# A two-layer graph kernel on one core: one-hot spans of 11 nodes per tile for 12

## What is computed

```python
deg = segment_sum(1, dst); mean(v) = segment_sum(v, dst) / max(deg, 1)
# layer 0
msg = (x[src] + rel_emb[type]) @ W_msg.T + b_msg
x   = layernorm(x + x @ W_self.T + b_self + mean(msg))
# layers 1 and 2, residual around both
h   = swish(mean(x[src]) @ W1_l.T + b1 + x @ W1_r.T)
out = layernorm(x + mean(h[src]) @ W2_l.T + b2 + h @ W2_r.T)
```

## Time and profile before

| | before |
|---|---|
| median of three runs | 349.58 us (349.37 to 349.80) |
| the profiled execution | 349.91 us, span 348.1 us |
| busy: TensorE | 326.0 us, 94% of the span |
| TensorE weight loads | 243.2 us |
| VectorE | 229.0 us, 66% |
| ScalarE | 176.7 us, 51% |
| GpSimd | 4.9 us |
| granted clock, mean | 0.99 |
| count of the first group starts | 11.33 us |
| last count ends | 167.74 us |

### The profile page before, as it was taken

How to read it: one execution, slowest core, us unless ns; L and a number is a source line. 1 busy time by engine, 2 the same in 40 slices (tenths; PEclk the granted TensorE clock), 3 DMA queues, 4 the chain that set the end, 5 groups by cost and what they waited for, 6 DMA issues and landing times.

```text
span 348.1 us, 9071 instructions
## 1 busy us (share of the span) xinstructions
PE 326.0 (94%) x3322; PEld 243.2 (70%) x3322; DVE 229.0 (66%) x592; ACT 176.7 (51%) x389; POOL 4.9 (1%) x18
## 2 busy tenths in 40 slices
PE   1689999999999999999999999999999999999990
PEld 0688799999999999999884654564564554554560
DVE  6989999999999999999337963303306315315404
ACT  3596787779779879779422431321332411220220
POOL 5000000000000000000000000000000000000000
PEclk9989999999999999999999999999999999999997
DMA  5702000000000000000200000000000011011011
GB/s 147 237 18 78 2 2 3 8 4 4 8 2 5 6 5 6 5 2 3 76 12 1 2 0 0 2 0 2 0 2 1 3 30 30 2 30 31 2 32 37
DMA packets 6957, 7.29 MB, mean 21 GB/s; under 512 B 653, under 2 KB 5888, under 8 KB 6912
## 3 DMA queue, kind: packets, MB, share of 16 engines
q1 hardware_dynamic: 6624, 6.25, 6.0%
q10 hardware_dynamic: 288, 0.43, 0.5%
HBM read 4.75 MB, written 1.60 MB: 18 GB/s over the span
## 4 chain that ended last, share of the span: by engine, by line
PE 87%; DVE 7%; ACT 1%; issue 1%; ACTq 0%; DVEq 0%
PE ps L1049 38%; PE ps L1030 18%; PE ps L975 18%; PE ps L1121 5%; PE ps L1131 3%; DVE hot L1286 2%; PE ps L1068 2%; DVE hot L1279 1%; PE ps L982 1%; DVE table L1296 1%; PE ps L992 1%; PE ps L1096 1%; ACT sum_first L828 1%; DVE table L1286 0%; PE ps L1012 0%
## 5 line engine op out<-in xcount | busy, mean ns | idle before, releaser
L1049 PE MATMUL ps<-counts,table 128*128 128x512 f16 (+1 forms) x736 | 135.2, 340 | 0.0
L910 ACT CAST counts<-ps 128x494 f32 x208 | 107.5, 576 | 33.5 <-PE ps L975 32.6
L1049 PEld LDWEIGHTS ps<-counts,table 128*128 128x128 f16 x736 | 60.6, 97 | 64.8 <-DVE table L1415 0.2
L1030 PE MATMUL ps<-counts,table 128*128 128x256 f16 x600 | 80.0, 271 | 1.0 <-ACT sum_first L828 0.8
L975 PE MATMUL ps<-hot 128*128 128x156 f16 (+1 forms) x592 | 67.7, 240 | 7.8 <-DVE hot L1286 7.6
L975 PEld LDWEIGHTS ps<-hot 128*128 128x128 f16 x592 | 53.1, 102 | 11.4 <-DVE hot L1286 9.6
L1286 DVE TENSOR_TENSOR hot<-iota,edges 128x1200 f16<-128x1200 f16 x74 | 57.3, 774 | 0.0
L1030 PEld LDWEIGHTS ps<-counts,table 128*128 128x128 f16 x600 | 52.0, 96 | 6.6 <-issue 1.3
L1279 DVE TENSOR_TENSOR hot<-iota,edge_rows 128x768 f16<-128x768 f16 x74 | 40.5, 548 | 3.1 <-PE ps L1012 2.7
L982 PE MATMUL ps<-window_hot,hot 128*128 128x19 f16 x296 | 42.5, 179 | 0.0
L851 ACT ACTIVATE scaled<-ps,rdeg 128x128 f32<-128x128 f32 (+1 forms) x75 | 21.7, 373 | 24.0 <-PE ps L1121 21.6
(11 more groups left out here) (149 smaller groups left out, 328.2 us busy)
## 6 DMA issues: line engine op xcount, KB each, us to landing
own_T<-x_turned SPq DMA_DIRECT2D x4, 256.0 KB, 2.6
table<-x_rows SPq DMA_DIRECT2D x1, 832.0 KB, 5.8
table<-x_rows SPq DMA_DIRECT2D x1, 768.0 KB, 4.2
out<-new_first SPq DMA_DIRECT2D x3, 256.0 KB
out<-hot SPq DMA_DIRECT2D x3, 256.0 KB, 2.3
sum_first<-x_turned SPq DMA_DIRECT2D x2, 256.0 KB, 4.4
counts<-counts SPq DMA_DIRECT2D x6, 53.0 KB
counts<-first_dst ACTq DMA_DIRECT2D x1, 208.0 KB, 3.6
```

The lines of the kernel that those rows point to most:

```text
L910: nc.scalar.copy(A[:, HALVES[half], bass.ds(bases[group % 8], GROUP_W)], window(group, half)).then_inc(copied[half], 1)
L1030: last = nc.tensor.matmul(ps[:, sums_bank(q), at:at + PART], table0[:, b, which, :], A[:, b, part * PART:(part + 1) * PART], start=k == 0, ...
L1049: last = nc.tensor.matmul(ps[:, sums_bank(q), 0:nodes], table[:, b, which, :], A[:, b, at:at + nodes], start=b == which == 0, stop=b + 1 = ...
```

## The change

TILE_W becomes 11. With it a tile's (block, node) row is 275 columns for 300 (L1286: 1100 for 1200 in a group), the block matmuls stream 143 and 132 columns for 156 and 144, `iota` has 550 elements for 600, MOST_SHIFT is 27 for 26, and the limits of the checks follow. A group's pair row is 531 columns for 556. `hot` then has 2124 words of four bytes for `later`, which held 2216; so `steps` (104 words) moves into `edge_rows`, and the last bias and the stacked identity move down by 104 words. With three lines added, line numbers behind it are larger by 3.

```diff
-TILE_W = 12
+TILE_W = 11
...
         checks = later[:, 4 * D + 2 * CHUNK:4 * D + 2 * CHUNK + TILES]
-        steps = later[:, 4 * D + 2 * CHUNK + TILES:4 * D + 2 * CHUNK + TILES + GROUPS]
-        bias_last = later[:, 4 * D + 2 * CHUNK + TILES + GROUPS:][:, 0:D]
-
-        ident_stacked = later[:, 5 * D + 2 * CHUNK + TILES + GROUPS:].bitcast(F16)[:, 0:LAST]
-        assert 5 * D + 2 * CHUNK + TILES + GROUPS + P // 4 <= (SLOTS - 1) * HOT_C * GROUP // 2
+        bias_last = later[:, 4 * D + 2 * CHUNK + TILES:][:, 0:D]
+
+        ident_stacked = later[:, 5 * D + 2 * CHUNK + TILES:].bitcast(F16)[:, 0:LAST]
+        assert 5 * D + 2 * CHUNK + TILES + P // 4 <= (SLOTS - 1) * HOT_C * GROUP // 2
+
+
+        edge_room = edge_row[:].rearrange("p h k t -> p (h k t)")
+        steps = edge_room[:, 2 * CHUNK:2 * CHUNK + 2 * GROUPS].bitcast(F32)
```

## The result

347.69 us is the median of six runs of the changed kernel (347.34 to 348.42), 349.48 that of six runs of the kernel before beside them (348.97 to 350.83): ratio 0.9953, 95% interval 0.9938 to 0.9968. The change is faster by 1.8 us. 345.4 was forecast with a range from 344.3 to 347.1: the sign was right, the size was not, and the range missed. The profiled execution took 347.51 us for a span of 345.6.

A forecast was written before the change was run, and what follows sets the result against it. TensorE was taken to bound the loop from 39.34 us, VectorE mostly before. Loop 3.35 plus start 0.9 gives 4.25, say 4.2 us off a 349.91 us profiled execution: 345.7, shifted 0.33 to the median, 345.4 us; range 344.3 to 347.1.

The forecast's parts named there:

- TensorE's count of a group: Counting loop: eight block matmuls lose 100 columns, 42 ns a group; over 87 groups 3.65 us.
- the sign that I had set for success: Trace of the count: the 128x143 matmul followed after 65 ns, with a count of 0.69 us.
- the loop's sum: TensorE-bound loop from group 17 on: 3.65 us by columns less 0.30 hidden by ScalarE, giving 3.35 us.
- What ScalarE keeps back of it: Loop: waits for ScalarE's copies hide three groups' saving, 0.13 us, and four at the share matmul, 0.17 us.
- The start: Before 40 us: VectorE's rows 0.58 plus TensorE's counts 0.55 less 0.22 for the low clock, 0.9 us.
- VectorE's part: One-hot rows, 53 ns less a group: worth nothing by itself where TensorE bounds, but needed to leave VectorE room.
- Parts at nothing: Moved steps and constants, shorter iota, pair row no longer a multiple of 16 bytes: all taken as zero cost.
- (a): Rival, loop: weight loads from uneven rows take half as long again, 78 ns a group; 352.1 us, 5%.
- (b): Rival, loop: written PSUM runs, not columns, set TensorE's pace, so only VectorE's 0.6 us stays; 349.0 us, 4%.
- (c): Rival, early chunks: ScalarE takes more, 25 groups gain nothing, 1.05 us for 0.30; 346.1 us, 12%.
- (d): Rival, before 40 us: the clock falls once more, giving back up to 1.7 us; 347.1 us, 5%.

The follow-up runs named there:

- e11: Kernel before with spans of 10 nodes, rows kept at 2224 bytes, leaving out the edge beyond; 343.69 us (one run).
- e3: Kernel before with spans of 8 nodes, rows kept at 2224 bytes, leaving out the edges beyond; 339.15 us (one run).
- e1: Changed kernel with one unused column between pair rows, pitch 2128 bytes for 2124; 347.55 us, ratio 0.9944 to the kernel before.
- e12: Kernel before, spans of 12, each tile's place rounded down to an even column; 348.18 us, ratio 0.9949 to the kernel before.
- e15: e1 with each tile's place rounded down to an even column; 346.68 us, ratio 0.9918 to the kernel before.
- e6: e1 with lighter ScalarE: early chunks' messages scaled by one instruction for four tiles, normalising cut to two columns; 346.65 us (one run).
- e5: TensorE alone narrowed to 11, VectorE still writing 1200 columns, rows 2224 bytes; 347.66 us, ratio 0.9945 to the kernel before.
- e2: Kernel before with one unused column between pair rows, pitch 2228 bytes for 2224, widths unchanged; 350.73 us (one run).
- e10: e1 with constant, mostly odd places (0, 9, 17, 25) instead of registers, so counts are wrong; 347.14 us (one run).
- e16: e15 with the four relation matmuls grouped behind the first half's four block matmuls; 346.31 us, ratio 0.9907 to the kernel before.

## Why the prediction was wrong, point by point

**The step that failed** is "TensorE's count of a group": eight block matmuls lose 100 columns at 0.42 ns, "I take 42". The slope came from matmuls that write contiguous columns. It nearly holds among even widths (38 and 39 ns for 100 columns in the medians of e11 and e3), but the step from 12 to 11 gives less. By the table of odd places, each odd place costs the kernel before 13 ns, two matmuls at 6.5; with 1.7 odd places in a group that is 23 ns above 702. At 11 columns a run has one odd end wherever it lies: at even places the count is 689 and not 702 - 42 = 660, so 29 ns are lost, and odd places add 6 each, 11 in all. With both ends called edges, these cost 23 ns before and 40 after; 42 - 17 = 25, and 728 - 702 = 26 is what e1 shows. Of the 42 ns, then, some 17 go to the edges, 2 to the pitch (a mean of 714 in e1, 716 after), about 7 to waits (the mean lies 5 ns above the median before, 12 after), and 17 were kept, as far as such differences add up.

What the runs show is the 29 ns, and the effect of the place; that the odd end is what costs the 29 is my inference. e11's runs of 10 have no odd end at even places, and there it gives back 68 ns for 200 columns (634 for 702), 16 short of 84. Against the middle of its even neighbours, 668 ns, 11 columns lose 21; the other 8 are open. Spacing by spacing, from e12 to e15, with all places even, the eight block matmuls give 27 ns (541 to 514, sums of median spacings) and the six short ones behind them take 16 back (159 to 175). So the sign that I had set for success, a 128x143 matmul followed after 65 ns, came nearly true (66) and told little: half of the loss sits behind the next matmul.

**Against the loop's sum.** 86 x 42 ns = 3.6 us were to be had by columns. Edges take 86 x 17 ns = 1.46, the pitch 0.2 (126.26 less 126.05), 1.31 were gained; some 0.6 are left, for which I had 0.30. "What ScalarE keeps back of it" was right for the share matmul: 0.2 us in the same four groups (0.47 to 0.67 us in the change), for 0.17. Another 0.2 us is lost in the five groups with late matmuls, where the prediction had nothing, and 0.1 us between the counts, where L1033's waits for ScalarE rose from 0.8 to 1.2 us. The first 0.2 is shown, by e6; the others are read from the traces and stay untried.

**The start** came out inside its bounds of 0.5 to 1.3, and not more can be said: 0.9 were forecast, 1.15 stand in the profile of the change, but its median time, 1.8 us less with 1.3 from the loop, leaves only 0.5. VectorE alone was timed at 0.65 us. L1289 takes 723 ns where 721 was forecast. That VectorE's part "is needed" for the loop was wrong (e5).

**Parts at nothing.** The steps' move cost nothing: 259 ns again, and 181.2 us of tail. The uneven pitch did not: I had taken A's rows for comparison, one moving operand at 256 columns, where the one-hot rows are also weights in front of short matmuls.

**The rivals.** (a) had the wrong size here (2 ns a group, not 78), though e2 shows 16 at 12 columns. (b) held the core of it, runs instead of columns, but I priced it as all or nothing, at 349.0, with 4%, against one row of 0.07 us which can't show a cost that is paid behind the next matmul. With half of the loop's 3.35 us lost it gives 0.9 + 1.7 = 2.6 us or 347.0, with two thirds 347.6; a range that reached to such a case would have come near the time. Beside it stood the Trainium skill, which (SBUF — State Buffer, section Specifications (TRN2)) gives PSUM lines of 8 bytes. The parity of the places agrees with pairs of floats; that a run of 11 costs as much as one of 12 does not: at even places 689 stands against 702. How the edges add up within a matmul (6.5 ns for two odd edges at 12, about 3.6 for one odd end, 6.7 when the odd edge is the first) no run here separates. (c) happened only in small part: its sign, waits for ScalarE over 2 us, was not met (1.2 and 0.3). (d) did not: the low stretch is as long as before.

**What the profile held.** Group 59 against 61, above, is in the trace of the kernel before. The same shapes at a different spacing were the sign that shape alone doesn't set the price.

## What to carry to other kernels

Before a cost by columns is applied to a matmul, look whether equal shapes have equal spacings in the trace; where they don't, find what differs (here the parity of the place in PSUM), and test an even width against an odd one. Even places were worth as much at 12 columns as the narrower span with odd runs; the two don't add up (each takes 26 or 27 ns off the median count, both together 40). A run that puts a constant in a register's place also drops the loads and the address arithmetic, so look in its trace for what else is gone. A rival whose mechanism can be partly true needs a price for the part.

## What the runs showed of the hardware that I had not expected

An f16 matmul that writes 12 or 13 runs of 12 floats into PSUM cost 6.5 ns more with the runs at an odd column than at an even one. A row pitch 4 bytes off cost 16 ns in a count of 15 matmuls at 12 columns, 2 ns at 11. The two surcharges don't add up: by the table of odd places, the pitch costs 25 ns at 12 columns where all places are even and some 5 where three are odd. At 11 columns the short matmuls already stand at 29 to 33 ns (e1). Why either costs anything is open.

The stretch at the clock's lower level moves between nearly equal kernels. After, it lies from 18.5 to 21.9 us; e5 has none; in e12 it is twice as long, from 19.6 to 26.5 us, and with it go a late group 17 (40.07 us) and the slowest of its six runs (349.19 us at a mean granted clock of 0.980, the others at 0.987 to 0.995). Windows of after, e5 and e12:

```profile
20.00:22.00 2.00, 1.91 (x24) 1.94 (x25) 1.65 (x5) 2.00 (x6) 0.00 (x0) 0.52 0.00 0
```

```profile
20.00:22.00 2.00, 1.77 (x26) 1.49 (x26) 1.69 (x5) 2.00 (x6) 0.00 (x0) 1.00 0.00 0
```

```profile
20.00:22.00 2.00, 1.73 (x22) 1.75 (x23) 1.59 (x4) 2.00 (x6) 0.00 (x0) 0.50 0.00 0
22.00:24.00 2.00, 2.00 (x17) 1.99 (x16) 2.00 (x5) 1.93 (x5) 0.00 (x0) 0.50 0.02 4
24.00:26.00 2.00, 2.00 (x23) 1.94 (x22) 0.53 (x2) 0.56 (x2) 0.00 (x0) 0.50 0.17 22
```

The second of these (e5) had waits like the others' before 20 us, so no row here says what decides. Over all versions with 11 columns group 17 starts between 38.19 and 39.30 us, and the stretch alone doesn't explain it: 38.19 in the change with 3.4 us of it, 38.26, 38.67 and 38.86 in e10, e5 and e16 without any. That is why the loop and the start are compared apart here, and why single times within 1 us of one another rank nothing.
